# The last product of a graph kernel cut at column 374, with a two-block last output group and the small stores moved to SyncE

## The reference

```python
h  = relu(layernorm(x))
for W, b in ((W0,b0),(W1,b1),(W2,b2)):          # three edge convolutions
    m = concat([h[dst], h[src]-h[dst]]) @ W + b
    h = relu(segment_sum(m, dst) / max(count, 1)) # each h is kept
x  = x + concat([h0,h1,h2,h3]) @ Wf + bf
h  = relu(layernorm(x))
agg = segment_sum(edge_weight * (h @ W4)[dst_of_edge], row) + b4
h   = (agg - mean(agg, nodes)) * rsqrt(var(agg, nodes) + 1e-5) * gamma + beta
out = x + relu(h)
```

## Time and profile before

| | |
|---|---|
| time, median of 3 runs (lowest to highest) | 111.09 us (110.65 to 111.28) |
| time of the profiled execution | 111.21 us |
| its span | 109.4 us |
| TensorE matmul busy | 98.6 us, 90% of the span |
| VectorE busy | 87.9 us, 80% |
| ScalarE busy | 63.8 us, 58% |
| GpSimd busy | 20.8 us, 19% |
| granted TensorE clock | 1.0 of full speed |
| bytes written to HBM | 0.64 MB |

### The profile page before, as it was taken

The page is one execution under the profiler, slowest core; times in us unless marked ns, Lnnn a source line. Parts: engine busy times, 40 slices in busy tenths (PEclk is TensorE's granted clock), DMA queues, the critical chain, the costliest instruction groups (busy, mean ns, idle before and its releaser), DMA issues.

```text
span 109.4 us, 2712 instructions
## 1 busy us (share of the span) xinstructions
PE 98.6 (90%) x1050; PEld 91.8 (84%) x1050; DVE 87.9 (80%) x257; ACT 63.8 (58%) x154; POOL 20.8 (19%) x27
## 2 busy tenths in 40 slices
PE   0395999979999999999999999999999999999950
PEld 0333898867799989999999999999999999999840
DVE  2589999999999998999953599940999989808960
ACT  1595999998699989302858133557513153423540
POOL 7200000000000059100399920192000000000000
PEclk9999999999999999999999999999999999999999
DMA  1984930000030000000050200000000000000035
GB/s 28 260 186 93 328 115 0 0 6 3 3 99 0 6 0 9 6 0 3 0 192 13 88 0 0 6 0 0 0 6 0 0 0 0 0 0 6 0 76 158
DMA packets 7008, 4.63 MB, mean 42 GB/s; under 512 B 2175, under 2 KB 6994, under 8 KB 6994
## 3 DMA queue, kind: packets, MB, share of 16 engines
q1 hardware_dynamic: 6068, 3.68, 12.4%
q10 hardware_dynamic: 926, 0.75, 2.6%
HBM read 3.79 MB, written 0.64 MB: 40 GB/s over the span
## 4 chain that ended last, share of the span: by engine, by line
PE 72%; DVE 17%; DMA 5%; issue 1%; ACTq 1%; ACT 0%; DVEq 0%
PE bank L1385 14%; PE bank L1286 12%; PE bank L1142 12%; PE bank L1143 11%; PE bank L1144 11%; DVE src_hot L591 8%; DMA x_in<-in_x_dram 5%; PE bank L1216 4%; PE bank L1423 2%; PE bank L1363 2%; DVE stats L544 2%; DVE stats L864 1%; PE bank L1468 1%; DVE x_in L895 1%; DVE dst_hot L587 1%
## 5 line engine op out<-in xcount | busy, mean ns | idle before, releaser
L591 DVE TENSOR_SCALAR src_hot<-node_id,edge_cols 125x626 f16<-125x626 f16 x77 | 23.6, 379 | 0.0
L1286 PE MATMUL bank<-dst_hot,src_hot 125*128 125x84 f16 (+6 forms) x505 | 20.1, 195 | 1.3 <-DVE src_hot L591 1.1
L1286 PEld LDWEIGHTS bank<-dst_hot,src_hot 125*128 125x128 f16 x505 | 18.8, 98 | 2.8 <-DVE src_hot L591 1.8
L1385 PE MATMUL bank<-counts,u_lo 125*128 125x312 f32 (+3 forms) x60 | 16.7, 308 | 0.0
L1068 ACT ACTIVATE h_hi<-pre 128x312 fp32r<-128x312 f32 (+1 forms) x12 | 5.6, 466 | 16.4 <-DVE pre L757 16.4
L1385 PE MATMUL bank<-counts,u_hi 125*128 125x312 f32 (+3 forms) x48 | 14.0, 307 | 0.0
L1143 PE MATMUL bank<-wf_hi,h_lo 128*125 128x256 f32 x40 | 11.3, 281 | 0.0
L1142 PE MATMUL bank<-wf_hi,h_hi 128*125 128x256 f32 x40 | 11.3, 281 | 0.0
L1144 PE MATMUL bank<-wf_lo,h_hi 128*125 128x256 f32 x40 | 11.2, 281 | 0.0
L1385 PEld LDWEIGHTS bank<-counts,u_lo 125*128 125x128 f32 (+1 forms) x60 | 11.0, 189 | 0.0
L1003 ACT ACTIVATE parts<-bank 125x250 f32<-125x250 f32 x25 | 10.2, 411 | 0.0
(11 more groups left out here) (144 smaller groups left out, 250.0 us busy)
## 6 DMA issues: line engine op xcount, KB each, us to landing
raw<-in_L_gnn_W_dram SPq DMA_DIRECT2D x3, 512.0 KB, 6.6
x_in<-in_x_dram ACTq DMA_DIRECT2D x1, 560.0 KB
raw<-in_L_gnn_Wf_dram SPq DMA_DIRECT2D x1, 512.0 KB, 3.7
out_dram<-x_in SPq DMA_DIRECT2D x2, 168.0 KB
wf<-in_L_gnn_Wf_dram SPq DMA_DIRECT2D x1, 256.0 KB, 7.6
raw<-in_L_gnn_Wf_dram SPq DMA_DIRECT2D x1, 256.0 KB, 2.7
raw<-in_L_gnn_W_dram SPq DMA_DIRECT2D x1, 256.0 KB, 2.7
out_dram<-x_in SPq DMA_DIRECT2D x2, 112.0 KB
```

The source lines that it names most:

```text
L591: dve.tensor_scalar(src_hot[:, t % RING, 0:IDS], node_id[:, 0:IDS], edge_cols[:, 0, t:t + 1], None, ALU.is_equal).then_inc(src_hot_vector, 1)
L1286: return pe.matmul(built[s][:, :, n0:n0 + n], src_hot[:, t % RING, BLK * s:BLK * s + P], dst_hot[:, c, :, j // 2, c0:c0 + n, j % 2], start ...
L1385: ins = pe.matmul(bank[KF * h + f][:, 0:e - a], u[0:n, k, P * f:P * (f + 1)], counts[0:n, k, a:e], start=False, stop=(k == NB - 1 and u is ...
```

## The change

The column halves of s and agg become 0 to 373 and 374 to 625. The halves of all earlier stages stay as they are. The output groups of feature half 1 become blocks 0, 1, 2 (y2) and blocks 3, 4 (y3); y2 stays with VectorE, and y3 is made like y0 and y1: x is put into its bank by TensorE ahead of y2's transposes, and ScalarE copies it out. SyncE issues the large store of y0, y1 and y2 and the small stores of all four groups; ScalarE issues only the large store of y3.

```diff
 HALVES = ((0, 312), (312, NODES_E))
+LAST_HALVES = ((0, 374), (374, NODES_E))
...
-        Y_GROUPS = [[(f, b) for b in blocks] for f in range(KF) for blocks in ((0, 1), (2, 3, 4))]
+        Y_GROUPS = [[(f, b) for b in blocks] for f, blocks in ((0, (0, 1)), (0, (2, 3, 4)), (1, (0, 1, 2)), (1, (3, 4)))]
+        Y_DONE = ((out_ready, 1), (out_ready, 2), (out_ready_vector, 1), (out_ready, 3))
...
# SyncE
-                sp.wait_ge(out_ready if i < 2 else out_ready_vector, i % 2 + 1)
-                sp.dma_start(to[0:FULL], x_in[0:FULL, b:b + n, P * f:P * (f + 1)]).then_inc(out_stored, 16)
+                sp.wait_ge(*Y_DONE[i])
+                if i < len(Y_GROUPS) - 1:
+                    sp.dma_start(to[0:FULL], x_in[0:FULL, b:b + n, P * f:P * (f + 1)]).then_inc(out_stored, 16)
+                sp.dma_start(to[FULL:BLK], x_in[FULL:BLK, b:b + n, P * f:P * (f + 1)]).then_inc(out_stored, 16)
...
# s_low, moments_of_agg, line 910 (VectorE); s_high, affine (ScalarE); s and agg loops (TensorE)
-                a, e = HALVES[h]
+                a, e = LAST_HALVES[h]
...
# VectorE, end
-            for i in range(2, len(Y_GROUPS)):
-                add_rows(i)
+            add_rows(2)
...
# ScalarE, end
-            for i, pairs in enumerate(Y_GROUPS):
-                f, b = pairs[0]
-                n = len(pairs)
-                to = out[BLK * b:BLK * (b + n), P * f:P * (f + 1)].rearrange("(b p) d -> p b d", p=BLK)
-                act.wait_ge(out_ready if i < 2 else out_ready_vector, i % 2 + 1)
-                act.dma_start(to[FULL:BLK], x_in[FULL:BLK, b:b + n, P * f:P * (f + 1)]).then_inc(out_stored, 16)
+            copy_out(3)
+            f, b = Y_GROUPS[-1][0]
+            to = out[BLK * b:NODES, P * f:P * (f + 1)].rearrange("(b p) d -> p b d", p=BLK)
+            act.wait_ge(*Y_DONE[-1])
+            act.dma_start(to[0:FULL], x_in[0:FULL, b:NB, P * f:P * (f + 1)]).then_inc(out_stored, 16)
...
# TensorE, output groups
             for i, pairs in enumerate(Y_GROUPS):
-                o = fill(("y", i)) if i >= 2 else groups.bank[("y", i)]
+                if i == 2:
+                    put_x(3)
+                o = fill(("y", i)) if i == 2 else groups.bank[("y", i)]
                 for n, (f, b) in enumerate(pairs):
                     to, rows = o[0:BLK, P * n:P * (n + 1)], pre_t[:, f, BLK * b:BLK * (b + 1)]
-                    if f:
+                    if i == 2:
                         pe.wait_ge(y_ready_vector, 1)
                     if b >= 2 or not f:
                         pe.wait_ge(y_ready, 3 if f else 1 if b < 2 else 2)
-                    if f:
+                    if i == 2:
                         ins = pe.transpose(to, rows, ident[:, :])
```

More of the change, by code:

```diff
@@ L909, in _ @@
             dve.wait_ge(scale_ready, 2)
-            a, e = HALVES[0]
+            a, e = LAST_HALVES[0]
             dve.tensor_scalar(pre_t[:, 1, a:e], groups.bank[("agg", AGG.index((1, 0)))][:, 0:e - a], scale[:, 1:2],
                               shift[:, 1:2], ALU.mult, ALU.add).then_inc(y_ready_vector, 1)
-            for i in range(2, len(Y_GROUPS)):
-                add_rows(i)
+            add_rows(2)
         @block.scalar
```

## The result

The kernel after takes 111.75 us, median of 6 runs (111.57 to 112.31), against 111.0 us for the kernel before (6 runs, 110.65 to 111.28). The ratio is **1.0077 [1.0054, 1.0099]**: slower by 0.75 us. The forecast was +0.24 us.

A forecast was written before the change was run, and what follows sets the result against it. The end was taken to be set by y1's issue and gaps in the output transfer. Terms: +0.15 us (y1's issue), +0.07 (gap), +0.02 (rounding) = +0.24, giving 111.3 us, range 110.7 to 111.8.

The forecast's parts named there:

- Step 1: Between s product and agg: TensorE stalls 0.19 us, waiting for the second s copy; bounds 0 to 0.26.
- Step 2: Agg and statistics: agg ends 0.19 us late, second statistics 0.06 shorter, so scale and shift come 0.14 later.
- Step 3: Scaling: L911 widens to 374 columns and ends 0.20 us later; y1 is issued 0.15 later, at 105.50.
- Step 4: put_x(3) on TensorE ahead of y2's transposes: its 0.48 us are hidden before L911's release, 0.1 to spare.
- Step 5: Output groups y2 and y3: y2 issued at 106.40 instead of 105.97, y3 at 106.67 instead of 106.43.
- Step 6: Small stores on SyncE: 0.41 us per queued issue, last issued at 107.22, landing at 108.7.
- beside, not behind: Step 6's claim that the last small store lands at 108.7, alongside the last large-store packets, without setting the end.
- Step 7, the transfer: Output transfer at 230 GB/s: 0.07 us gap before y2's data, finishing at 108.64 instead of 108.40.
- Step 7, its two constants: End of run: 0.96 us from 108.4 to span end, and profiled time 111.21 + 0.24, median 0.12 lower.
- the slow pace of 252 columns: Rival in s and agg: 42 matmuls take 0.24 instead of 0.116 us, +5.2 us, 116.3; chance 0.03.
- The transfer did not cover anything: Rival on the output transfer: a rate nearer 297 GB/s covers the delay or gains, -0.5 to +0.1 us; chance 0.26.
- the second rival: Large stores y2 and y3 overlap in two queues at 169 GB/s: in all +0.65 us, 111.7; chance 0.11.

The follow-up runs named there:

- after_split_wait: The kernel after, with agg's first two groups waiting for one s copy at a time; ratio 1.0058 against the kernel before.
- small_on_sync: The kernel before, with SyncE issuing each small store behind its large one instead of ScalarE; ratio 1.0055 against the kernel before.
- after_vector_same_length: The kernel after with one dummy copy at VectorE's end, making 257 VectorE instructions as in the kernel before; ratio 1.0046 against the kernel before.
- last_large_on_scalar: The kernel before, with y3's large store issued by ScalarE and its small one by SyncE; ratio 0.9992 against the kernel before.
- groups_only: The kernel after with the cut back at column 312 and the old store engines (SyncE large, ScalarE small); ratio 1.0040 against the kernel before.

## Why the prediction was wrong, step by step

Times of the prediction are shifted by 0.36.

- **Step 1, stall: right.** The second s copy ends at 98.39 (forecast 98.79, shifted 98.43). The s product's last matmul starts at 98.31 and would be followed at 98.43. The first agg matmul of 374 columns streams until the next one starts at 98.78, so it began streaming at 98.78 - 0.17 = 98.61 (its record, at 98.53, is early). Stall 0.18; forecast 0.19. after_split_wait shows that the wait for the second copy is its cause.
- **Step 2: right.** The second statistics start at 100.55 against 100.38: +0.17 (forecast +0.20), and take 0.43 instead of 0.49.
- **Step 3: right within 0.06.** L915 (the old L911) ends at 104.69 against 104.53: +0.16 (forecast +0.20). y1 is issued at 105.08 against 104.99: +0.09 (forecast +0.15).
- **Step 4: right.** put_x(3) starts at 104.24 and the transposes at 104.83, 0.14 after L915's end: its release decides, as before.
- **Step 5: right.** y2 is issued at 106.01, +0.40 (forecast +0.43); y3 at 106.28, +0.21 (forecast +0.24).
- **Step 6: right for the queue.** The last small store is issued at 106.87 (forecast 107.22, shifted 106.86). small_on_sync shows what the forecast did not price, since it kept y3's large store out of that queue: 0.87 us per pair. But "beside, not behind" fails, most likely. SyncE's queue ends at 108.62, ScalarE's with y3's large store at 108.49. The last packets of SyncE's queue are three rows of 512 bytes and one packet of 4, then two rows and one packet of 4: y2's small store has three rows to a partition and y3's two, and y3's was issued last. So the last packet fits y3's small store, which the forecast named as a sign that it was wrong. It costs at most those 0.13 us.
- **Step 7, the transfer: mechanism right, size low.** The gap is there (116 GB/s for 0.2 us, so about 0.1 us idle; forecast 0.07), and the last packet is at 108.62 against the shifted 108.28: +0.34, forecast +0.24. Counted from the first s matmul, after is 0.07 us behind with 450 KB still to move, 0.23 with 300 KB, and 0.34 at the end: the late y1, the gap, and 0.11 on the last 300 KB, for which the forecast had no term. The forecast took 230 GB/s throughout, but before ran at 266 GB/s from 107.6 to 108.2, and after at 224 from 106.9 to 108.2.
- **Step 7, its two constants: the step that failed.** "From 108.4 to the end of the span it takes 0.96 us more" was carried over unchanged. Counted from the last packet, that time grew from 0.72 to 0.92: +0.20, nearly all of it ahead of the last count of the stores (0.34 to 0.53 us). And "Profiled time 111.21 + 0.24" took the 1.85 us around the span as fixed: they grew to 2.18, +0.33 in the profiled pair and +0.37 by the medians. 0.24 + 0.10 + 0.20 = 0.54 is the tail's growth, and with 0.37 it is 0.91; the medians hold 0.75 of it. With the part outside undone, after_vector_same_length still lost 0.53 us by its medians (1.0046 [1.0028, 1.0063]): twice the +0.24, at the upper edge of the forecast's +0.1 to +0.5. So the terms of the span were too low as well, and the time outside was missing altogether.

The rivals: the slow pace of 252 columns is dead (0.12 us from the start of one to what follows, 98.36 to 98.48 in the rows of after_split_wait: full pace). With y2 in one queue and y3 in the other, from 107.5 to 108.2, no tenth of a microsecond of after fell under 195 GB/s, and last_large_on_scalar is not slower. The transfer did not cover anything. The 0.11 us on the last 300 KB may be a small share of that rival; no run takes it apart. None of the rivals was what happened in the main: all of them were in the span. The chance for a loss over 0.5% was put at 0.15, for mechanisms that were not the one. The measured 111.75 lies inside the stated 110.7 to 111.8 only because the range took in the price of the second rival, which did not occur: that is luck.

On the receipt from memory: the last packet after is followed by 0.92 us in which the DMA engines do nothing (most of it is the last window, 108.70 to 109.50). The Trainium skill ("DMA: Bandwidth & Descriptors", section "Anatomy of one DMA") puts most of about 2.0 us of fixed cost of a DMA on another issue path into that receipt. The stores of this case agree only in part: 0.85 us pass from issue to data and 0.32 to 0.61 from the last packet to the last count, 1.2 to 1.5 us in all, and the receipt is the smaller part. The 1.5 us by which the forecast spoke against the page ran only up to the last packet, not to the count.

## What to carry to other kernels

When a change is worth a few tenths of a microsecond, compare run time minus span over several runs before explaining anything by the trace: it may hold half of the difference, as here, and it can follow the instruction count of one engine. The trace's semaphore records behind the last instruction show in which step it lies. To see what an edit does by itself, keep that count, if need be with a tiny dummy instruction at the engine's end, and read times from a marker that the change does not touch. A wider first group in a chain of groups makes the next stage wait for its copies, unless the wait is for one copy at a time; a pair of stores on one queue delays the next store by two issues.

## What the runs showed of the hardware that was not expected

- Time outside the span by VectorE's instruction count: 2.16 to 2.23 us at 256 (10 kernels), 1.80 to 1.84 at 257 (8 kernels), 1.96 and 1.97 at 258. It is not monotonic. It lies in the closing sequence of semaphore updates behind the last instruction: fifth to sixth update 0.47 us at 256, 0.10 or 0.11 at 257 and 258. No run tells why the count decides; kernels with other counts were not tried.
- Four idle-time matmuls fewer at the start (groups_pe_shorter) cost 0.7 us in the span (109.9 against 109.2 for groups_only, on different chips); the profiles show 0.37 us, ahead of the first s matmul.
- A small store holds the issuing queue about as long as a large one. Issued after a pause, both take 0.32 to 0.39 us. Issued right behind another on the same queue, a store takes 0.43 to 0.49 in some places (small ones behind their large one in small_on_sync, y3's large one in groups_only) and 0.35 to 0.38 in others (y2's large one in small_on_sync, y3's small one in after). Size does not decide it.
- From the last packet to the end of the span it takes 0.71 to 1.06 us in these kernels, which all write the same number of bytes. The part behind the last count is 0.38 or 0.39 us in 18 of the 20.
